# A fused cross-attention and mixture-of-experts kernel: the first loads over two queues, K of batch 0 by halves, and a block that closes without GpSimd's drain

## The chip, the core and the metric

The kernel runs as one program on one core of a Trainium2 chip. Its engines are TensorE (PE), VectorE (DVE), ScalarE (ACT), GpSimd (POOL) and SyncE (SP). They run their own instruction streams and meet at semaphores; DMAs are issued from the queues of SyncE, ScalarE and GpSimd. The metric is the device time of one execution in microseconds.

## The reference

x and the context have 4 batches of 512 tokens of 256 features, in f32. Every line below is computed.

```python
kv = (mem @ W_kv)                       # layernorm(x) and mem = ctx: 16 heads of 16
q = (x @ W_q)
attn = softmax(q k^T * HEAD_DIM ** -0.5)
x = x + tanh(g_xattn[0]) * ((attn @ v) @ W_proj + b_proj)
logits = xf @ gate_w.T                  # xf = layernorm(x), 2048 tokens, 8 experts
topk_logits, topk_idx = jax.lax.top_k(logits, 2)
topk_w = softmax(topk_logits)
for e in range(8):
    out = out + comb[:, e:e+1] * ((silu(xf @ wg[e].T) * (xf @ wu[e].T)) @ w_down[e].T)
x = x + tanh(g_ffn[0]) * (shared + out)  # shared: the same gated form with its own weights
```

## The kernel before

The program is one block in which each engine's instructions stand in an order written out by hand; nothing schedules them. It has three stages.

The first stage, some 60 us, loads ctx (already transposed on the host, `ctxT`), x and the attention weights, normalises x by batch, and makes K, V and Q of each batch. SyncE's queue carries the K half of `w_kv`, ctxT of batch 0, the V half, and then ctxT and x of batches 1 to 3. ScalarE's queue carries x of batch 0, `w_q`, the two gates, the bias, `w_proj` and the router weights. TensorE first runs `WARM` = 36 transposes of an identity tile whose result nobody reads (L1290). Then, for batches 0 and 1, it runs `project_k` (two output halves c, each a sum over two input halves d), half of `project_v`, `turn_xn` (eight transposes of the normalised rows `rows` into xnT, L1300), the other half of `project_v`, and `project_q`. All plain products go through the helper `mm` at L1284.

K and Q of batches 0 and 1 are each split into three bf16 parts. ScalarE makes the high part from PSUM (`high_k`, L701; `high_q`, L697), VectorE the residual (`resid_part`, L923), ScalarE the middle part (`mid_part`, L689), and VectorE the low part (`low_part`, L913). ScalarE also copies the turned rows (`copy_xnT`, L693) and V (`copy_v`, L709), takes standard deviations (`std_of`, L677) and, for batches 1 to 3, applies the normalisation (`apply_rows`, L683), all in one fixed order. Next to these VectorE has the statistics of x (`ln_stats`, L880 and L884), and for batch 0 the whole normalisation (`ln_apply`, ending at L894). `project_k(b, 0)` waits for ctxT of its batch (`ctx_in`) and, for batches 1 and 2, for the residual of the batch before, since both use the same PSUM banks. For batches 2 and 3 K and Q are copied whole (`whole_k`, L714; `whole_q`, L718). From batch 2 on, score tiles for the row maxima of the first unit (`first_pair`) stand between the products; VectorE reduces each pair (`max_pair`, L929), and from the third pair on TensorE waits for the maximum before last.

SyncE copies the parts of batch 0 into the units' operands (48 DMAs, `copy_rows`, L430, from the low part of K on), then stores the parts of batch 1 (L444), then sends the first row maxima (`send_max`, L457), for which the first unit's scores wait.

The second stage is the attention of 16 units (a batch and four heads), paced by TensorE. The third is projection, router, shared expert and 36 expert blocks. GpSimd adds each block's rows to `out` in HBM by indirect DMAs (L655). SyncE waits for all of them at the end (L502). At the block's end every engine drains, and all meet in a barrier (L143).

Of the kernel before, what the change touches and what calls it, by code (L numbers as in the profile page):

```python
# [22 lines left out]
P = 128  # L23
# [5 lines left out]
B, T, D = 4, 512, 256  # L29
N = B * T  # L30
NT = N // P
TB = T // P
DC = D // P
# [5 lines left out]
E, HALF, FFN = 8, 384, 768  # L39
# [45 lines left out]
ROW_HOMES = 8  # L85
EPS = 1e-5
GATE_W = P // TB
WARM = 36

K_RUNS = ((0, 1, 2), (0,), (0, 1))  # L90
Q_RUNS = ((0, 1), (0, 1, 2), (0,))
# [43 lines left out]
def build(nc, x, ctxT, g_xattn, g_ffn, w_kv, w_q, w_proj, b_proj, gateT, w_upT, w_downT, out):  # L135
# [4 lines left out]
    x_dram = x.rearrange("b (t p) d -> p (b t) d", p=P)  # L140
    out_dram = out[0:N, :].rearrange("(t p) d -> p t d", p=P)

    with ExitStack() as ctx:  # L143
        def sb(name, shape, dt=F32):
            return ctx.enter_context(nc.sbuf_tensor(name, shape, dt))

        def sem(name):
            return ctx.enter_context(nc.semaphore(name))

        x_sb = sb("x_sb", [P, NT, D])
# [3 lines left out]
        ctx_sb = ctx_region[:, :].rearrange("p (c n) -> p c n", c=DC)  # L155
# [5 lines left out]
        dn_region = sb("dn_region", [P, (E + 1) * FC * D])  # L161
        w_dn = dn_region[:, :].rearrange("p (e f n) -> p e f n", e=E + 1, f=FC)
        part_words = B * 2 * 3 * DC * T // 2
        parts = up_region[:, 0:part_words].bitcast(BF16).rearrange("p (b a j c n) -> p b a j c n", b=B, a=2, j=3, c=DC)
        resid = dn_region[:, 0:2 * DC * T].rearrange("p (a c n) -> p a c n", a=2, c=DC)
        v_words = TB * H * VW

        unit_words = 4 * HG * T + v_words
# [80 lines left out]
        wkv_sb = sb("wkv_sb", [P, DC, 2 * D])  # L249
        wp_sb = sb("wp_sb", [P, DC, D])  # L250
        gate_sb = sb("gate_sb", [P, DC, GATE_W])
        bias_sb = sb("bias_sb", [P, D])
# [3 lines left out]
        ident = sb("ident", [P, P])  # L256
# [47 lines left out]
        def bank(i, n=1):  # L304
            return ps[i // 4][:, i % 4, :] if n == 1 else ps[i // 4][:, i % 4:i % 4 + n, :]
# [4 lines left out]
        K_BANK, V_BANK = 4, 6  # L310
# [9 lines left out]

        x_in = [sem(f"x_in{b}") for b in range(B)]
        ctx_in = [sem(f"ctx_in{b}") for b in range(B)]
        wk_in, wv_in, wq_in = sem("wk_in"), sem("wv_in"), sem("wq_in")
        gates_in = sem("gates_in")
        small_in = sem("small_in")
        const_step = sem("const_step")
        gate_zero = sem("gate_zero")
# [16 lines left out]
        k_ps, v_ps, q_ps = sem("k_ps"), sem("v_ps"), sem("q_ps")  # L344
# [53 lines left out]
        out_done = sem("out_done")  # L398

        order_steps = [0]  # L400
        block = ctx.enter_context(nc.Block())

        @block.sync
        def _(sp):
            def load_ctx(b):
                sp.dma_start(ctx_sb[:, :, b * T:(b + 1) * T],
                             ctxT.rearrange("(c p) n -> p c n", p=P)[:, :, b * T:(b + 1) * T]).then_inc(ctx_in[b], 16)

            w_kv_rows = w_kv.rearrange("(c p) n -> p c n", p=P)  # L410
            sp.dma_start(wkv_sb[:, :, 0:D], w_kv_rows[:, :, 0:D]).then_inc(wk_in, 16)
            load_ctx(0)
            sp.dma_start(wkv_sb[:, :, D:2 * D], w_kv_rows[:, :, D:2 * D]).then_inc(wv_in, 16)
            for b in range(1, B):
                load_ctx(b)
                sp.dma_start(x_sb[:, b * TB:(b + 1) * TB, :], x_dram[:, b * TB:(b + 1) * TB, :]).then_inc(x_in[b], 16)

            def load_rows(b, g, a, dst, runs):
                row = 0
# [239 lines left out]

        @block.scalar  # L660
        def _(act):
            act.dma_start(x_sb[:, 0:TB, :], x_dram[:, 0:TB, :]).then_inc(x_in[0], 16)
            act.dma_start(wq_sb[:, :, :], w_q.rearrange("(c p) n -> p c n", p=P)).then_inc(wq_in, 16)
            act.dma_start(gates[:, 0:1], g_xattn.partition_broadcast(P)).then_inc(gates_in, 16)
            act.dma_start(gates[:, 1:2], g_ffn.partition_broadcast(P)).then_inc(gates_in, 16)
            act.dma_start(bias_sb[:, :], b_proj.partition_broadcast(P)).then_inc(small_in, 16)
            act.dma_start(wp_sb[:, :, :], w_proj.rearrange("(c p) n -> p c n", p=P)).then_inc(small_in, 16)
            act.wait_ge(gate_zero, 1)
            act.dma_start(gate_sb[:, :, 0:E], gateT.rearrange("(c p) n -> p c n", p=P)).then_inc(small_in, 16)

            def copy_first_max():
                act.wait_ge(nmT_ps, 1)
# [199 lines left out]

        @block.vector
        def _(dve):
            nc.vector.memset(gate_sb[:, :, :], 0.0).then_inc(gate_zero, 1)
            nc.vector.memset(eps_sb[:, :], EPS)

# [49 lines left out]
            def max_pair(w, p, s):  # L927
# [8 lines left out]
            nc.vector.tensor_copy(same_e_bf[:, :], same_e[:, :])  # L936
            nc.vector.tensor_copy(before_tile[:, :, :],
                                  same_e[:, :].unsqueeze(1).to_broadcast([P, NT, E])).then_inc(route, 1)
            dve.wait_ge(x_in[0], 16)
            ln_stats(0, 1)  # L940
            ln_apply(0, 1)
            resid_part(1, 0)
# [146 lines left out]
            for t in range(NT):  # L1089
                last = nc.vector.max(top8[:, t, :], logits[:, t, :])  # L1090
# [5 lines left out]
            for t in range(NT):  # L1096
                last = nc.vector.max_index(top8_idx[:, t, :], top8[:, t, :], logits[:, t, :])
# [3 lines left out]
            for k in range(TOPK):  # L1101
                last = nc.vector.tensor_tensor(onehot[:, k, :, :], topi[:, k, :].unsqueeze(2).to_broadcast([P, NT, E]),
                                               iota_e[:, :].unsqueeze(1).to_broadcast([P, NT, E]), ALU.is_equal)
# [73 lines left out]
            for i in range(TABLE_PARTS):  # L1177
                n = PAIRS // TABLE_PARTS
# [103 lines left out]
        def _(pe):  # L1282
            def mm(o_, w, m, start=True, stop=True):
                return nc.tensor.matmul(o_, w, m, start=start, stop=stop)  # L1284

            pe.wait_ge(ident_done, 1)

            for i in range(WARM):
                nc.tensor.transpose(bank(7)[:, 0:P], ident[:, :], ident[:, :])  # L1290

            def turn_xn(b):
                pe.wait_ge(rows_done, b + 1)
                if b == 1:
                    pe.wait_ge(rowsT_sb, 1)
                elif b >= 2:
                    pe.wait_ge(whole_sb, WHOLE_ORDER.index((1, b)) + 1)
                for t in range(TB):
                    for c in range(DC):
                        last = nc.tensor.transpose(bank(XT_BANK[b] + c)[:, t * P:(t + 1) * P],  # L1300
                                                   rows[:, b * TB + t, c * P:(c + 1) * P], ident[:, :])
                last.then_inc(rowsT_ps, 1)

            def project_q(b, c, chunks=range(DC)):
                if (c, chunks[0]) == (0, 0):
                    if b == 0:
                        pe.wait_ge(wq_in, 16)
                    pe.wait_ge(rowsT_sb, b + 1)
                    if b == 1:
                        pe.wait_ge(resid_done, QK_ORDER.index((0, 0)) + 1)  # L1310
                    elif b >= 2:
                        pe.wait_ge(v_done, b + 1)
                for d in chunks:
                    last = mm(bank(Q_BANK[b] + c), wq_sb[:, d, c * P:(c + 1) * P], xnT[:, d, b * T:(b + 1) * T],
                              d == 0, d == DC - 1)
                if (c, chunks[-1]) == (DC - 1, DC - 1):
                    last.then_inc(q_ps, 1)

            def project_k(b, c):
                if c == 0:  # L1320
                    if b == 0:
                        pe.wait_ge(wk_in, 16)
                    pe.wait_ge(ctx_in[b], 16)
                    if b in (1, 2):
                        pe.wait_ge(resid_done, QK_ORDER.index((1, b - 1)) + 1)
                    elif b == 3:
                        pe.wait_ge(rowsT_sb, 3)
                for d in range(DC):
                    last = mm(bank(K_BANK + c), wkv_sb[:, d, c * P:(c + 1) * P], ctx_sb[:, d, b * T:(b + 1) * T],
                              d == 0, d == DC - 1)  # L1330
                if c == DC - 1:
                    last.then_inc(k_ps, 1)

            def project_v(b, tiles):
                if tiles[0] == 0:
                    if b == 0:
                        pe.wait_ge(wv_in, 16)
                    elif b <= 2:
                        pe.wait_ge(v_done, b)
                    else:  # L1340
                        pe.wait_ge(whole_sb, WHOLE_ORDER.index((0, 2)) + 1)
                for kt in tiles:
                    for d in range(DC):
                        tok = b * T + kt * P
                        last = mm(bank(V_BANK + kt // 2)[:, (kt % 2) * D:(kt % 2 + 1) * D], ctx_sb[:, d, tok:tok + P],
                                  wkv_sb[:, d, D:2 * D], d == 0, d == DC - 1)
                if tiles[-1] == TB - 1:
                    last.then_inc(v_ps, 1)
# [61 lines left out]
                            max_tile(u + 2, kt * HG + i, w, lambda p: True)  # L1410
                    also(k)

            for b in range(2):
                project_k(b, 0)
                project_k(b, 1)
                project_v(b, (0, 1))
                turn_xn(b)
                project_v(b, (2, 3))
                project_q(b, 0)
                project_q(b, 1)  # L1420

            def first_pair(w, p):
                if p == 0:
# [363 lines left out]
```

## Time and profile before

| | us |
|---|---|
| median of 3 runs | 493.08 |
| the 3 runs | 493.06 to 493.8 |
| profiled execution | 493.61 |
| its span, first to last instruction | 491.9 |
| TensorE busy | 476.5 (97%) |
| VectorE, ScalarE, GpSimd busy | 305.9, 261.0, 183.9 |

The span is 1.71 us shorter than the profiled execution's own time. Busy shares are averages over stages; the change lies in the first 60 us and behind the last 10 us, so the rows further down come from those two places.

### The profile page before, as it was taken

Reading aid. Unit: us, or ns where it says so; the run is one execution under the profiler, and the core shown is the slowest. Engines: PE = TensorE matmul, PEld = TensorE weight load, DVE = VectorE, ACT = ScalarE, POOL = GpSimd, SP = SyncE. Lnnn points to the kernel's source line nnn. Section 1 sums busy time; section 2 is a strip of 40 time slices with the busy share of each in tenths; the row PEclk is TensorE's granted clock in tenths of the full one; section 3 lists DMA queues with packets and bytes.
Section 4 is the critical chain, followed back from the end, with each engine's and each line's share of the span. In section 5 each row is a group of like instructions: output and inputs, shape, how many; then the busy total and the mean of one; then the engine's idle time right before and its main releaser. Section 6 shows DMA issues by size and latency. Waiting matters only on the chain.

```text
span 491.9 us, 7745 instructions
## 1 busy us (share of the span) xinstructions
PE 476.5 (97%) x2783; PEld 286.3 (58%) x2783; DVE 305.9 (62%) x574; ACT 261.0 (53%) x416; POOL 183.9 (37%) x216
## 2 busy tenths in 40 slices
PE   8999999999999999999989999999999999999992
PEld 7665523333233233334446465699799799799992
DVE  3666779999899999996464699533333333333331
ACT  1665277777777777776544400306346346244430
POOL 4810178872231111111000023604547647767332
PEclk9999999999999999999999999999999999999997
DMA  7733408866753565211104001322334525445232
GB/s 246 236 102 105 138 7 228 218 182 183 212 147 87 159 165 163 65 34 55 33 24 149 1 2 43 113 93 46 63 53 65 76 45 87 65 63 78 33 33 32
DMA packets 36741, 48.30 MB, mean 98 GB/s; under 512 B 6240, under 2 KB 29920, under 8 KB 36704
## 3 DMA queue, kind: packets, MB, share of 16 engines
q1 hardware_dynamic: 21536, 26.16, 18.8%
q0 software_dynamic: 7344, 9.84, 13.1%
q10 hardware_dynamic: 7824, 11.81, 7.6%
q8 instruction: 23, 0.38, 0.4%
q14 instruction: 14, 0.11, 0.1%
HBM read 30.16 MB, written 14.29 MB: 90 GB/s over the span
## 4 chain that ended last, share of the span: by engine, by line
PE 94%; DVE 3%; ACT 1%; issue 1%; POOLq 0%; POOL 0%
PE ps L1284 73%; PE ps L1370 13%; PE ps L1646 2%; PE ps L1657 2%; PE ps L1290 1%; PE ps L1679 1%; DVE rows L894 1%; DVE neg_max L929 1%; ACT ctx_region L763 1%; PE ps L1300 1%; PE ps L1362 0%; PE ps L1518 0%; PE ps L1527 0%; POOLq L143 0%; DVE stats L880 0%
## 5 line engine op out<-in xcount | busy, mean ns | idle before, releaser
L763 ACT ACTIVATE ctx_region<-ps 128x512 f32<-128x512 f32 x256 | 140.7, 594 | 47.5 <-PE ps L1284 47.5
L929 DVE TENSOR_REDUCE neg_max<-ps 128x2 f32<-128x1024 f32 x128 | 151.0, 1209 | 21.5 <-PE ps L1284 19.6
L1284 PE MATMUL ps<-unit_region 96*128 96x512 bf16 (+1 forms) x512 | 128.4, 380 | 1.2 <-ACT ctx_region L763 0.7
L1284 PEld LDWEIGHTS ps<-unit_region 96*128 96x128 bf16 (+1 forms) x512 | 45.0, 97 | 101.4 <-ACT ctx_region L763 45.2
L1284 PE MATMUL ps<-unit_region,ctx_region 128*128 128x128 f32 (+1 forms) x824 | 97.4, 274 | 0.0
L1284 PEld LDWEIGHTS ps<-unit_region,ctx_region 128*128 128x128 f32 (+1 forms) x824 | 94.3, 188 | 0.7 <-DVE x_sb L1071 0.3
L655 POOL DMA_INDIRECT out<-unit_region x39 | 61.2, 1570 | 54.2 <-DMA out<-unit_region 31.0
L1284 PE MATMUL ps<-dn_region,unit_region 128*128 (+1 forms) x294 | 70.0, 381 | 0.0
L844 ACT COPY ctx_region<-up_region 128x1536 f32 x33 | 48.5, 1472 | 34.8 <-PE ps L1284 27.2
L1241 DVE TENSOR_TENSOR unit_region<-unit_region,ps 128x384 f32<-128x384 f32 x35 | 19.4, 555 | 71.5 <-ACT unit_region L861 62.6
L1284 PEld LDWEIGHTS ps<-dn_region,unit_region 128*128 128x128 f32 x294 | 53.2, 190 | 8.4 <-issue 2.8
L861 ACT ACTIVATE unit_region<-ps 128x384 f32<-128x384 f32 x36 | 17.6, 490 | 63.5 <-PE ps L1284 59.2
L1370 PE MATMUL ps<-ctx_region,dn_region 128*32 128x512 f32 x384 | 51.1, 605 | 0.0
L622 POOL DMA_INDIRECT rows<-x_rows,unit_region x36 | 36.0, 1000 | 34.5 <-DMA out<-x_sb 13.5
L578 POOL CAST nm_parts<-nmT 16x128 bf16<-16x128 f32 x16 | 4.5, 280 | 114.8 <-ACT nmT L755 100.6
L1284 PE MATMUL ps<-xnT,up_region 128*128 128x512 f32 x96 | 42.6, 595 | 0.0
L1262 DVE TENSOR_SCALAR unit_region<-ps,unit_region 128x256 f32<-128x256 f32 x36 | 17.4, 484 | 27.2 <-PE ps L1284 23.3
L628 POOL TENSOR_TENSOR unit_region<-ctx_region,unit_region 128x1248 bf16<-128x1248 bf16 x3 | 8.0, 2652 | 63.1 <-DVE ctx_region L1163 63.0
L1284 PEld LDWEIGHTS ps<-xnT,up_region 128*128 128x128 f32 x96 | 17.8, 190 | 19.8 <-issue 19.7
L805 ACT ACTIVATE unit_region<-ps 128x512 f32<-128x512 f32 x12 | 7.0, 596 | 28.6 <-PE ps L1284 28.6
L1370 PEld LDWEIGHTS ps<-ctx_region,dn_region 128*32 128x32 f32 x384 | 7.5, 108 | 18.9 <-ACT ctx_region L763 14.9
L1370 PE MATMUL ps<-ctx_region,unit_region 128*32 128x512 f32 x128 | 17.0, 605 | 0.8 <-ACT ctx_region L763 0.8
(200 smaller groups left out, 464.8 us busy)
## 6 DMA issues: line engine op xcount, KB each, us to landing
up_region<-in_w_upT ACTq DMA_DIRECT2D x9, 768.0 KB, 4.5
qk_parts<-up_region SPq DMA_DIRECT2D x24, 192.0 KB, 3.2
unit_region<-qk_parts SPq DMA_DIRECT2D x24, 192.0 KB, 4.1
dn_region<-in_w_downT ACTq DMA_DIRECT2D x9, 384.0 KB, 5.3
unit_region<-up_region SPq DMA_DIRECT2D x48, 64.0 KB, 2.6
unit_region<-qk_parts SPq DMA_DIRECT2D x24, 128.0 KB, 4.1
ctx_region<-in_ctxT SPq DMA_DIRECT2D x4, 512.0 KB, 10.4
x_rows<-rows SPq DMA_DIRECT2D x4, 512.0 KB, 3.9
```

Of the source, the lines that this page charges most:

```text
L622: pool.indirect_dma_start(out=blk_x[:, home, :], out_offset=None, in_=x_rows[:, :], in_offset=bass.IndirectOffsetOnAxis(ap=blk_token[:, AD ...
L655: pool.indirect_dma_start(out=out[:, :], out_offset=bass.IndirectOffsetOnAxis(ap=blk_row[:, a:a + 1], axis=0), in_=blk_y[:, j % Y_HOMES, : ...
L763: nc.scalar.activation(probs[:, k % 8, :], bank(SCORE_HOME[u, k]), ACT.Exp).then_inc(exp_done, 1)
L844: nc.scalar.copy(up_now[:, n % 2, :, :].rearrange("p c f -> p (c f)"), w_up[:, bass.ds(chosen_expert.pop(a), 1), :, :].rearrange("p a c f ...
L861: nc.scalar.activation(blk_gate[:, :], bank(2 * (j % 2))[:, 0:HALF], ACT.Silu).then_inc(bsilu, 1)
L929: nc.vector.tensor_reduce(neg_max[:, s, 2 * p:2 * p + 2], bank(2 * (p % 2), 2), AX.X, ALU.max, negate=True).then_inc(max_done, 1)
L1241: nc.vector.tensor_tensor(blk_h[:, s, :], blk_gate[:, :], bank(2 * s + 1)[:, 0:HALF], ALU.mult).then_inc(bhid, 1)
L1262: nc.vector.tensor_scalar(blk_y[:, j % Y_HOMES, :], bank(6 + s)[:, 0:D], blk_weight[:, ADDS_OF[j][0]:ADDS_OF[j][0] + 1], None, ALU.mult).t ...
L1284: return nc.tensor.matmul(o_, w, m, start=start, stop=stop)
L1370: last = nc.tensor.matmul(bank(6)[h * VW:(h + 1) * VW, :], v_home(u // NG)[:, kt, u % NG * HG + h, :], probs[:, (kt * HG + h) % 8, :], sta ...
L1646: last = nc.tensor.transpose(bank(4)[:, c * P:(c + 1) * P], blk_x[:, s, c * P:(c + 1) * P], ident[:, :])
L1657: nc.tensor.matmul(bank(2 * s + g)[0:HALF_P, 0:HALF], blk_xT[:, s, c, 0:HALF_P], w_up[:, bass.ds(expert[ADDS_OF[j][0]], 1), c, cols].rearr ...
```

## The change

(2) SyncE's queue starts with ctxT of batch 0 in two halves by input feature, each with its own semaphore, then the first tile of x, then the V weights. (3) ScalarE's queue starts with the K weights in two halves, then the other three tiles of x of batch 0; the bias, `w_proj` and the router weights move to SyncE, behind its other loads and ahead of the copies. (4) The first K products run by input half: both output halves for d = 0, then both for d = 1, in two PSUM banks. (5) The warm-up is nine plain f32 matmuls of a zeroed 128x128 piece of `dn_region`, behind a memset of VectorE, in place of 36 transposes of the identity. (6) V of batch 0 is made in one piece ahead of the turn of xn. (7) K of batch 1 is split: its first output half goes between the turn and Q of batch 0, its second behind Q.

```diff
-WARM = 36
+WARM = 9
-        block = ctx.enter_context(nc.Block())
+        block = ctx.enter_context(nc.Block(no_gpsimd_drain=True))
...
-            sp.dma_start(wkv_sb[:, :, 0:D], w_kv_rows[:, :, 0:D]).then_inc(wk_in, 16)
-            load_ctx(0)
-            sp.dma_start(wkv_sb[:, :, D:2 * D], w_kv_rows[:, :, D:2 * D]).then_inc(wv_in, 16)
+            for c in range(DC):
+                sp.dma_start(ctx_sb[:, c, 0:T], ctxT[c * P:(c + 1) * P, 0:T]).then_inc(first_ctx_in[c], 16)
+            sp.dma_start(x_sb[:, 0:1, :], x_dram[:, 0:1, :]).then_inc(x_in[0], 16)
+            sp.dma_start(wkv_sb[:, :, D:2 * D], w_kv.rearrange("(c p) n -> p c n", p=P)[:, :, D:2 * D]).then_inc(wv_in, 16)
...
+            sp.dma_start(bias_sb[:, :], b_proj.partition_broadcast(P)).then_inc(small_in, 16)
+            sp.dma_start(wp_sb[:, :, :], w_proj.rearrange("(c p) n -> p c n", p=P)).then_inc(small_in, 16)
+            sp.wait_ge(gate_zero, 1)
+            sp.dma_start(gate_sb[:, :, 0:E], gateT.rearrange("(c p) n -> p c n", p=P)).then_inc(small_in, 16)
...
-            act.dma_start(x_sb[:, 0:TB, :], x_dram[:, 0:TB, :]).then_inc(x_in[0], 16)
+            for c in range(DC):
+                act.dma_start(wkv_sb[:, c, 0:D], w_kv[c * P:(c + 1) * P, 0:D]).then_inc(wk_in[c], 16)
+            act.dma_start(x_sb[:, 1:TB, :], x_dram[:, 1:TB, :]).then_inc(x_in[0], 16)
...
+            nc.vector.memset(warm[:, :], 0.0).then_inc(warm_set, 1)
...
-            dve.wait_ge(x_in[0], 16)
+            dve.wait_ge(x_in[0], 16 * 2)
...
+            pe.wait_ge(warm_set, 1)
+            for i in range(WARM):
+                mm(bank(7)[:, 0:P], warm[:, :], warm[:, :])
             pe.wait_ge(ident_done, 1)
-
-            for i in range(WARM):
-                nc.tensor.transpose(bank(7)[:, 0:P], ident[:, :], ident[:, :])
...
+            def project_first_k():
+                for d in range(DC):
+                    pe.wait_ge(wk_in[d], 16)
+                    pe.wait_ge(first_ctx_in[d], 16)
+                    for c in range(DC):
+                        last = mm(bank(K_BANK + c), wkv_sb[:, d, c * P:(c + 1) * P], ctx_sb[:, d, 0:T], d == 0, d == DC - 1)
+                last.then_inc(k_ps, 1)
```

On TensorE, from its first instruction to Q of batch 0, this stood in the program before (`ident` is the identity tile, `wkv_sb` the K and V weights, `ctx_region` ctxT, `xnT` the turned rows):

```order
L1290 MATMUL ps<-ident 128x128 [waits ident_done]
L1290 MATMUL ps<-ident 128x128 x35
L1284 MATMUL ps<-ctx_region,wkv_sb 128x512 [waits ctx_in0,wk_in]
L1284 MATMUL ps<-ctx_region,wkv_sb 128x512 x3
L1284 MATMUL ps<-wkv_sb,ctx_region 128x256 [waits wv_in]
L1284 MATMUL ps<-wkv_sb,ctx_region 128x256 x3
L1300 MATMUL ps<-ident,rows 128x128 [waits rows_done]
L1300 MATMUL ps<-ident,rows 128x128 x7
L1284 MATMUL ps<-wkv_sb,ctx_region 128x256 x4
L1284 MATMUL ps<-xnT,wq_sb 128x512 [waits rowsT_sb,wq_in]
```

And this stands there now, on the same engine, up to the second half of K of batch 1:

```order
L1290 MATMUL ps<-dn_region 128x128 [waits warm_set]
L1290 MATMUL ps<-dn_region 128x128 x8
L1290 MATMUL ps<-ctx_region,wkv_sb 128x512 [waits first_ctx_in0,wk_in0,ident_done]
L1290 MATMUL ps<-ctx_region,wkv_sb 128x512
L1290 MATMUL ps<-ctx_region,wkv_sb 128x512 [waits first_ctx_in1,wk_in1]
L1290 MATMUL ps<-ctx_region,wkv_sb 128x512
L1290 MATMUL ps<-wkv_sb,ctx_region 128x256 [waits wv_in]
L1290 MATMUL ps<-wkv_sb,ctx_region 128x256 x7
L1306 MATMUL ps<-ident,rows 128x128 [waits rows_done]
L1306 MATMUL ps<-ident,rows 128x128 x7
L1290 MATMUL ps<-ctx_region,wkv_sb 128x512 [waits resid_done,ctx_in1]
L1290 MATMUL ps<-ctx_region,wkv_sb 128x512
```

The turn of the rows (L1300, now L1306) has moved behind all eight V products, and the first half of K of batch 1, with its wait for the residual, has moved ahead of Q.

On SyncE's queue, the first loads stood like this, up to the first copy of the parts:

```order
L411 DMA wkv_sb<-in_w_kv 128x2x256
L407 DMA ctx_region<-in_ctxT 128x2x512
L413 DMA wkv_sb<-in_w_kv 128x2x256
L407 DMA ctx_region<-in_ctxT 128x2x512
L416 DMA x_sb<-in_x 128x4x256
L407 DMA ctx_region<-in_ctxT 128x2x512
L416 DMA x_sb<-in_x 128x4x256
L407 DMA ctx_region<-in_ctxT 128x2x512
L416 DMA x_sb<-in_x 128x4x256
L430 DMA unit_region<-up_region 16x4x512 [waits low_done]
```

Now the same queue has:

```order
L414 DMA ctx_region<-in_ctxT 128x512 x2
L415 DMA x_sb<-in_x 128x256
L416 DMA wkv_sb<-in_w_kv 128x2x256
L410 DMA ctx_region<-in_ctxT 128x2x512
L419 DMA x_sb<-in_x 128x4x256
L410 DMA ctx_region<-in_ctxT 128x2x512
L419 DMA x_sb<-in_x 128x4x256
L410 DMA ctx_region<-in_ctxT 128x2x512
L419 DMA x_sb<-in_x 128x4x256
L420 DMA bias_sb<-in_b_proj 128x256
L421 DMA wp_sb<-in_w_proj 128x2x256
L423 DMA gate_sb<-in_gateT 128x2x8 [waits gate_zero]
```

The K weights have left this queue for ScalarE's, a tile of x stands ahead of the V weights, and three loads of ScalarE's queue stand at its end.

## Rows read from the trace of the kernel before

**Rows 1.** The page: the chain that ended last, its shares of the span by engine.

```profile
PE 94%; DVE 3%; ACT 1%; issue 1%; POOLq 0%; POOL 0%
```

**Rows 2.** The chain in order of time: start us, us, engine and line; first and later pieces.

```profile
1.58 6.83 PE ps L1290 x36
8.41 5.16 PE ps L1284 x16
...
37.71 11.22 PE ps L1284 x36
```

**Rows 3.** The timeline, 0 to 12 us: start us, us, engine, line, operation.

```profile
0.89 0.11 DVE L875 MEMSET gate_sb<- 128x64 f32 x1 [0.89 <-PEq L1780]
...
1.31 0.45 SPq L407 DMA_DIRECT2D ctx_region<-in_ctxT  x1
...
5.74 1.41 DVE L880 BATCH_NORM_STATS2 stats<-x_sb 128x6 f32<-128x256 f32 x4 [3.46 <-DMA x_sb<-in_x]
...
8.14 1.38 DVE L894 TENSOR_SCALAR rows<-x_sb,mean_var,rstd 128x256 f32<-128x256 f32 x4
...
8.25 3.60 PE L1284 MATMUL ps<-ctx_region,wkv_sb 128*128 128x512 f32 x8
...
11.69 1.89 PE L1284 MATMUL ps<-wkv_sb,ctx_region 128*128 128x256 f32 x8
```

**Rows 4.** Warm-up alone: busy time in one window, and its weight loads, 6 to 6.5 and 7.2 to 8 us.

```profile
2.00:6.90 4.90, 4.90 (x25) 4.90 (x24) 1.00 0.92 306
...
L1290 PEld LDWEIGHTS ps<-ident 128*128 128x128 f32 x3 | 0.7, 230 | 0.0
...
L1290 PEld LDWEIGHTS ps<-ident 128*128 128x128 f32 x8 | 0.9, 140 | 0.0
```

**Rows 5.** Windows from the start; the last numbers are clock, DMA share and GB/s.

```profile
0.00:4.10 4.10, 2.52 (x12) 2.52 (x13) 0.81 (x5) 0.00 (x0) 2.74 (x14) 1.00 0.40 123
0.00:5.50 5.50, 3.92 (x19) 3.92 (x20) 0.81 (x5) 0.25 (x1) 2.86 (x14) 1.00 0.57 188
0.00:6.30 6.30, 4.72 (x22) 4.72 (x23) 1.37 (x7) 1.05 (x1) 2.86 (x14) 1.00 0.63 208
```

**Rows 6.** DMA issues of 0 to 1.5 us: size, us from issue to landing.

```profile
x_sb<-in_x ACTq DMA_DIRECT2D x1, 512.0 KB, 4.9
ctx_region<-in_ctxT SPq DMA_DIRECT2D x1, 512.0 KB, 6.3
wkv_sb<-in_w_kv SPq DMA_DIRECT2D x1, 256.0 KB, 3.8
```

**Rows 7.** The timeline, ScalarE's copy of the turned rows of batch 0.

```profile
14.49 1.01 ACT L693 COPY xnT<-ps 128x1024 f32<-128x1024 f32 x1 [1.59 <-PE ps L1300]
```

**Rows 8.** The timeline, 29 to 43 us: ScalarE, VectorE and TensorE around the first maxima.

```profile
29.19 2.08 ACT L683 ACTIVATE rows<-x_sb,shift,rstd 128x256 f32<-128x256 f32 x4 [0.44 <-DVE shift L908]
...
35.75 3.66 DVE L929 TENSOR_REDUCE neg_max<-ps 128x2 f32<-128x1024 f32 x3
...
37.55 0.60 PE L1284 MATMUL ps<-unit_region 96*128 96x512 bf16 x2
...
42.50 1.23 DVE L929 TENSOR_REDUCE neg_max<-ps 128x2 f32<-128x1024 f32 x1 [0.93 <-PE ps L1284]
```

**Rows 9.** The end, by line: count, ns min/median/max, first and last start.

```profile
L502 SPq EVENT_SEMAPHORE  x2: 17/22/28, 487.8 to 487.8; - x2
...
L143 POOLq DRAIN  x1: 7968/7968/7968, 483.7 to 483.7; - x1
...
L143 SPq DRAIN  x1: 7/7/7, 488.1 to 488.1; - x1
```

**Rows 10.** The timeline: SyncE's queue from 17 us, and TensorE's last max tiles and first scores.

```profile
17.73 31.26 SPq L430 DMA_DIRECT2D unit_region<-up_region  x48
...
54.50 14.48 SPq L457 DMA_DIRECT2D unit_region<-nm_parts  x6
...
60.90 1.03 PE L1284 MATMUL ps<-unit_region 96*128 96x512 bf16 x4
```

More of the change, by code:

```diff
@@ L165, in build @@
         resid = dn_region[:, 0:2 * DC * T].rearrange("p (a c n) -> p a c n", a=2, c=DC)
+        warm = dn_region[:, 0:P]
         v_words = TB * H * VW
@@ L322, in build @@
         ctx_in = [sem(f"ctx_in{b}") for b in range(B)]
-        wk_in, wv_in, wq_in = sem("wk_in"), sem("wv_in"), sem("wq_in")
+        first_ctx_in = [sem(f"first_ctx_in{c}") for c in range(DC)]
+        wk_in = [sem(f"wk_in{c}") for c in range(DC)]
+        wv_in, wq_in, warm_set = sem("wv_in"), sem("wq_in"), sem("warm_set")
         gates_in = sem("gates_in")
@@ L408, in load_ctx @@
                              ctxT.rearrange("(c p) n -> p c n", p=P)[:, :, b * T:(b + 1) * T]).then_inc(ctx_in[b], 16)
-            w_kv_rows = w_kv.rearrange("(c p) n -> p c n", p=P)
-            sp.dma_start(wkv_sb[:, :, 0:D], w_kv_rows[:, :, 0:D]).then_inc(wk_in, 16)
-            load_ctx(0)
-            sp.dma_start(wkv_sb[:, :, D:2 * D], w_kv_rows[:, :, D:2 * D]).then_inc(wv_in, 16)
+            for c in range(DC):
+                sp.dma_start(ctx_sb[:, c, 0:T], ctxT[c * P:(c + 1) * P, 0:T]).then_inc(first_ctx_in[c], 16)
+            sp.dma_start(x_sb[:, 0:1, :], x_dram[:, 0:1, :]).then_inc(x_in[0], 16)
+            sp.dma_start(wkv_sb[:, :, D:2 * D], w_kv.rearrange("(c p) n -> p c n", p=P)[:, :, D:2 * D]).then_inc(wv_in, 16)
             for b in range(1, B):
@@ L665, in _ @@
             act.dma_start(gates[:, 1:2], g_ffn.partition_broadcast(P)).then_inc(gates_in, 16)
[L666 to L669, printed above, removed]
             def copy_first_max():
@@ L1317, in project_q @@
                     last.then_inc(q_ps, 1)
+            def project_first_k():
[5 more added lines that the diff above has]
+                last.then_inc(k_ps, 1)
             def project_k(b, c):
                 if c == 0:
-                    if b == 0:
-                        pe.wait_ge(wk_in, 16)
                     pe.wait_ge(ctx_in[b], 16)
@@ L1411, in slot @@
                     also(k)
[L1413 to L1420, printed above, removed]
+            project_first_k()
+            project_v(0, (0, 1))
+            project_v(0, (2, 3))
+            turn_xn(0)
+            project_k(1, 0)
+            project_q(0, 0)
+            project_q(0, 1)
+            project_k(1, 1)
+            project_v(1, (0, 1))
+            turn_xn(1)
+            project_v(1, (2, 3))
+            project_q(1, 0)
+            project_q(1, 1)
             def first_pair(w, p):
```

## The prediction

> **What bounds the kernel now.** I read the chain that ended last first. It gives TensorE 94% of 491.9 us [rows 1], so only two kinds of time are to be had: time before TensorE's first useful product, and time after its last. In order of time the chain starts with the 36 warm-up transposes (1.58 to 8.4 us) and goes straight into the K products of batch 0. From there to 48.9 us TensorE has no gap, apart from pieces that the chain gives to itself [rows 2]. The rows of the first microseconds show what the start waits for: the warm-up itself. The last piece that the K products need, ctxT of batch 0, is issued at 1.31 and lands 6.3 us later, at 7.6; the K products begin at 8.25 behind the last transpose [rows 3, 6]. At the other end the last scatter-add has landed by 487.8 us, where SyncE's wait ends, and SyncE's own drain is over at 488.1. But the drain of GpSimd runs from 483.7 for 7.97 us, to 491.7, and the closing barrier stands behind it [rows 9]. The profiled execution took 493.61 us, 1.71 more than its span and 0.53 more than the median of the three runs.
>
> **The closing step.** The new program has no such drain for GpSimd; the other four keep theirs. What is late next is SyncE at 488.1; its wait for all scatter-adds stays. In the old program 0.2 us passes between the drain's end (491.7) and the end of the span, and I keep that: 488.3 in place of 491.9, a gain of **3.6 us**. Bounds: 3.6 if nothing outside the span takes over, and 0 if what follows the kernel has to do the same drain. I take 3.6, since every byte has landed and no row after 487.8 shows work. The Trainium skill ("Runtime: NRT & Kernel Launch", The ~15µs preamble/postamble breakdown) has a barrier and a DMA re-arm behind every kernel. By that page GpSimd might be waited for there, and the gain would be 0; no row here shows that stretch.
>
> **The start of TensorE.** Cold, the transposes follow each other every 0.213 us (25 records of 0.42 us overlap 4.9 us), later about twice as fast; their weight loads go from 230 to 140 ns, and 36 records in 6.57 us fit 25 slow ones, so TensorE went from 1.2 to 2.4 GHz at about 7.1 us [rows 3, 4]. (The profile's clock column has 1.00 for all of it and does not tell the two apart.) The new warm-up is nine plain f32 matmuls. A plain f32 matmul leaves two records (four K products are eight [rows 3]), so 18 records, 18 x 0.213 = 3.85 us. They wait for a small memset of VectorE, whose first one starts at 0.89, not for ident at 1.52: start about 1.1, end about 5.0.
>
> **The first loads.** Counting bytes by stretches of the windows view, 504 KB had moved by 4.1 us, 1034 by 5.5, 1310 by 6.3 [rows 5]. x of batch 0 (512 KB, alone at the head of ScalarE's queue) landed at 5.7, when 1.1 MB had moved in all, so the two queues shared about equally, and a landing shows 0.2 to 0.6 us behind its bytes (the first weights, issued at 0.80, took 3.8 us; their 256 KB are through at about 4.1) [rows 5, 6]. New order: SyncE has a 256 KB ctxT half, the second half, one x tile, V weights; ScalarE has two 128 KB weight halves, three x tiles, wq. So the first halves are in at about 4.6, the second at about 5.9, x of batch 0 (640 KB on each queue) at about 6.7, 1 us later than before, V weights (896 KB) at about 8.5. K can start right behind the warm-up, at 5.0, and its second half, wanted at 7.5 at the earliest, never waits. The Trainium skill ("DMA: Bandwidth & Descriptors", Issuing engines are not separate DMA queues) says that transfers issued by several engines run on the same 16 DMA engines and interleave. By it the second queue brings no bandwidth at all. The rows agree: both queues together stay at about the rate of the windows [rows 5], and my landings use that rate; what changes is only which bytes go first.
>
> **K and what follows it.** K takes 3.44 us at the high clock (8.25 to 11.69 [rows 3]). Started at 5.0 with the rise at 7.1, half of those 2.1 us is lost: K ends at 5.0 + 3.44 + 1.05 = 9.5, **2.2 us** earlier. The rise may come 1.5 us either way (the trace has one sample): 0.75 each way. All eight V products now run before the turn of xn: 12.95. The turn (0.87) wants the normalised rows: VectorE needed 3.8 us from the landing of x to the end of its rows (5.74 to 9.52 [rows 3]), so 10.5, early enough. It ends at 13.8; before, the copy of the turned rows on ScalarE began at 14.49 [rows 7], now about 14.05. So ScalarE and VectorE are ahead by 0.45 only, TensorE by 2.2, and the slack between them shrinks. Moving K(1, 0) behind the turn covers that copy: it ends at 15.1, Q wants it at 15.5. I followed the order of both engines with the durations of the old rows. Q of batch 0 ends at 19.0, its high part on ScalarE at 20.7, the residual at 22.0, copy_xnT(1) at 25.0, just when TensorE wants it (25.05). The residual of K(1) is through at 25.6 and its mid part at 26.7 (before 27.64), so apply_rows(2) runs from 28.25 (before 29.19). From there ScalarE is ahead by 0.9: the high part of Q(1) right behind it, and the first row maximum at VectorE from 34.95 (before 35.8, three of them in 3.66) [rows 8]. TensorE, 2.1 ahead, is at the turn of batch 2 by 34.55 and at its third pair of score tiles by 35.45. That pair waits for the first maximum, 1.2 us long: 36.2. Before, it began at 37.55 [rows 8]. **So 0.8 us of the 2.1 is given back to VectorE's first maxima; 1.3 stays.** From there on the distances stay, since TensorE with its products between the pairs is slower per pair than VectorE, which waited 0.93 us for it between maxima of 1.23 [rows 8].
>
> **SyncE.** It issues from 17.73 without a pause: 48 copies to 49.0, 8 stores, and then the three rows of maxima from 54.5, which land about 2.6 us later each, the last near 58 [rows 10]. The moved loads (bias, wp, gate) stand ahead of the copies; bytes in all are the same, and the queue must be free by 17.3, when the low part of K is due. Before, its last initial issue was over at 9.6; I expect 13 to 14. The first scores stand right behind the last max tiles, at about 61.3 [rows 10], now 60.0: still 2 us of slack. No cost. ScalarE is free of these three issues sooner; its table load only moves ahead. bias is first read behind the maxima of the second unit and wp in the last units, far later. No cost either.
>
> **Sum.** 493.61 - 3.6 - 1.3 = 488.7 against the profiled execution, 488.2 against the median. I say 488.4.
>
> **Rivals.**
> (a) The front gain stays whole: the rise of the clock comes early, or VectorE's maxima don't hold. 2.1 to 2.6 us: 487.3. For it: before, no wait at all showed there. Against: the third pair began at 37.55 and the first maximum was over by 37.0 [rows 8], a distance of 0.6 us.
> (b) The front gain is lost: x lands at 9 or later instead of 6.7, or the rise comes near 9, and ScalarE's chain starts no earlier than now. 489.6 to 489.9.
> (c) The drain comes back behind the span. The span shrinks to 487, the time does not: 493.3 - 1.3 = 492.0.
> (d) Both (b) and (c): 493.2, no change.
> (e) Slower: TensorE's clock stays at 1.2 GHz much longer, since the K, V and turn work now has gaps around the loads where an unbroken row of 36 transposes stood. With the rise at c the useful work done by c is (c - 5.0)/2 against c - 8.25 before; less 3.6 for the end, it is slower from c = 18.7 us on, and with (c) from c = 11.5 on. At c = 14 with (c): 494.3. Against: TensorE is busy without a gap from 1.1 to the turn by my landings.
>
> **How the numbers follow.** Forecast (487.8 to 489.1) 0.54; (a) 0.16; (b) 0.10; (c) 0.12; (d) 0.04; (e) 0.04. A measurement of this kernel can tell about 0.2%, 1 us, from no change. Faster: forecast, (a), (b), (c) = 0.92; same: (d) = 0.04; slower: 0.04. Without (c) to (e), 0.2 is left out, so the range is 486.6 to 490.4, which takes in (b) and an early rise.
>
> **What would show it.** Right: no long GpSimd drain at the end, span ending 0.5 us behind SyncE's last wait, time minus span still 1.7; K products from about 5.0, half speed until about 7; a wait of TensorE on VectorE's maximum near 35.5. Wrong: time minus span of 5 us (c); a wait of TensorE ahead of the turn of xn (b); weight loads of 230 ns in the V products (e); maxima for the first scores landing after 60 (SyncE late).

## The result, and the profile after

| | before | after |
|---|---|---|
| median | 493.07 us | 488.72 us |
| runs | 492.94 to 493.8 | 488.55 to 488.92 |
| ratio, 95% interval | | 0.9909 (0.9892 to 0.9926) |
| profiled execution | 493.61 us | 488.55 us |
| its span | 491.9 us | 486.5 us |
| time minus span | 1.71 us | 2.05 us |

The kernel is 4.35 us faster, 0.9%. I had forecast 488.4 between 486.6 and 490.4.

First the end, which answers to [rows 9]. These are rows of the kernel after by line, with count, ns and start:

```profile
L143 POOLq EVENT_SEMAPHORE  x2: 17/17/17, 486.3 to 486.4; - x2
...
L143 SPq DRAIN  x1: 7/7/7, 486.2 to 486.2; - x1
```

GpSimd has no drain any more. SyncE's drain starts at 486.2, and the last semaphore instruction stands at 486.4. Before, 3.8 us lay between SyncE's drain (488.1) and the end of the span; now it is 0.3.

Then the first microseconds, the timeline of the kernel after, which answers to [rows 3] and [rows 7]:

```profile
1.12 4.20 PE L1290 MATMUL ps<-dn_region 128*128 128x128 f32 x18 [1.12 <-DVE dn_region L880]
...
5.71 3.67 PE L1290 MATMUL ps<-ctx_region,wkv_sb 128*128 128x512 f32 x8 [0.40 <-DMA wkv_sb<-in_w_kv]
...
8.98 1.41 DVE L886 BATCH_NORM_STATS2 stats<-x_sb 128x6 f32<-128x256 f32 x4 [6.70 <-DMA x_sb<-in_x]
...
9.77 3.72 PE L1290 MATMUL ps<-wkv_sb,ctx_region 128*128 128x256 f32 x16 [0.39 <-DMA wkv_sb<-in_w_kv]
...
11.38 1.38 DVE L900 TENSOR_SCALAR rows<-x_sb,mean_var,rstd 128x256 f32<-128x256 f32 x4
...
13.33 1.04 PE L1306 MATMUL ps<-ident,rows 128*128 128x128 f32 x8
...
14.40 1.01 ACT L698 COPY xnT<-ps 128x1024 f32<-128x1024 f32 x1 [2.38 <-PE ps L1306]
```

K starts 2.54 us earlier than before (8.25), at 5.71. But x lands 3.2 us later (8.98 against 5.74), the V products wait for their weights until 9.77, and the turn of xn at 13.33 is where it was (13.41). ScalarE's copy of the turned rows starts at 14.40 against 14.49.

And the place where TensorE meets VectorE's first maxima, the timeline of the kernel after from 32 to 38.5 us, which answers to [rows 8]:

```profile
34.43 0.60 PE L1290 MATMUL ps<-unit_region 96*128 96x512 bf16 x2
34.87 1.04 PE L1306 MATMUL ps<-ident,rows 128*128 128x128 f32 x8
34.97 3.48 DVE L935 TENSOR_REDUCE neg_max<-ps 128x2 f32<-128x1024 f32 x3
...
36.24 0.60 PE L1290 MATMUL ps<-unit_region 96*128 96x512 bf16 x2 [0.33 <-DVE neg_max L935]
```

The third pair of score tiles starts at 36.24, 1.31 us earlier than before (37.55), and behind a wait for VectorE's first maximum that the kernel before did not have.

The difference of the two profiled executions, 5.06 us, has four parts that the rows show: 1.31 at the start; about 0.4 from a stall near 130 us that only the execution of before has (last section); 3.5 at the end of the span; less 0.34 that shows between span and time. They add up to 4.9; where the other 0.1 to 0.2 lies I did not find.

### The profile page after: what moved, and what is told of

The parts are those of the page before. It is cut to its first block, busy times and chain, and to the rows that moved or that the text cites. A ratio compares the mean times of both kernels' runs of the same rounds, so it can differ in the third digit from the quotient of the medians.

```text
span 486.5 us, 7717 instructions
## 1 busy us (share of the span) xinstructions
PE 474.4 (98%) x2765; PEld 283.5 (58%) x2765; DVE 305.7 (63%) x575; ACT 260.9 (54%) x416; POOL 183.9 (38%) x216
## 4 chain that ended last, share of the span: by engine, by line
PE 88%; DVE 5%; ACT 3%; DMA 2%; issue 1%; POOL 0%; SPq 0%; POOLq 0%
PE ps L1290 69%; PE ps L1382 13%; PE ps L1663 2%; PE ps L1674 2%; DMA wkv_sb<-in_w_kv 2%; DVE neg_max L935 1%; PE ps L1696 1%; ACT up_region L694 1%; ACT rows L688 1%; DVE dn_region L929 1%; DVE rows L900 1%; ACT ctx_region L768 1%; PE ps L1374 0%; PE ps L1535 0%; PE ps L1544 0%
```

## The experiments

All kernels of the study have one addition: GpSimd checks the bounds of the counts that it loads for its scatter-adds. The first run is the kernel before with that addition, the second the changed kernel. They are the two controls. The kernels came in three groups, each with the kernel before measured beside it: its median was 492.93 us beside the first four, 492.68 beside the next four (old order, old loads, whole operands, V weights first) and 492.74 beside the last four. So a difference of 0.2 us between kernels of different groups can be one of the groups.

**Control of before.** 

> The kernel before with one addition that all kernels of this study have: GpSimd checks the bounds of the counts that it loads for the scatter-adds. A control. If that addition lies off the path, 493.1 us (492.9 to 493.8). If GpSimd is on the path between the scatter-adds, up to 1 us more.

Measured: 493.26 us (ten runs, 492.73 to 493.68); the kernel before itself beside it 492.93. Ratio 1.0005 (0.9995 to 1.0014). The addition costs nothing that can be measured. In its profile K starts at 7.82, not at 8.25, right behind the landing of ctxT (7.7), since TensorE's weight loads went to the high clock at 5.9 us and not at 7.1: the old warm-up ends a little earlier or later from execution to execution.

**Control of after.** 

> The changed kernel with the same addition, a control. 488.7 us, and 4.35 below the control of before. The 0.5 us stall of TensorE near 130 us that the profiled execution of before shows and that of after doesn't is by chance, if it is in one of these two profiles or in neither, whichever.

Measured: 488.77 us (488.3 to 488.88), 4.49 below the control of before. The stall near 130 us is in this profile, although it is not in the one of the changed kernel.

**The closing step alone.**

```diff
-        block = ctx.enter_context(nc.Block())
+        block = ctx.enter_context(nc.Block(no_gpsimd_drain=True))
```

> The kernel before, and only the closing step without GpSimd's drain. My theory (two separate gains, 3.55 in the span at the end less 0.35 that shows outside it, 1.3 at the start): 489.85, span 488.3, time minus span 2.05. Rival (the end is worth all of it, and what TensorE gained at the start is swallowed before the end): 488.7.

Measured: 489.43 us (489.05 to 490.27), ratio to before 0.9925 (0.9909 to 0.9942): 3.8 us below the control, 0.7 above the changed kernel. The rows of its end by line:

```profile
L502 SPq EVENT_SEMAPHORE  x2: 17/22/28, 487.9 to 487.9; - x2
...
L143 SPq DRAIN  x1: 7/7/7, 488.2 to 488.2; - x1
```

The span is 488.4: it ends 0.5 us behind SyncE's last wait. Time minus span was 1.76 to 1.87 in its four runs, against 1.73 to 1.88 in the ten of the control. So nothing took over outside the span. This is rival (c) of the prediction, and it falls. The 0.34 of the two profiled executions is not all scatter, though. Time minus span is 1.77 in the mean of the control of before, 1.82 in the mean of each of the two kernels that have one part of the change, and 1.86 to 2.01 in the means of the ten kernels that have both. Some 0.1 to 0.2 us of the gain in the span is thus lost outside it once both parts are in. What it goes to no row shows.

**The start alone**: the changed kernel with `nc.Block()`. 

> The changed kernel, but GpSimd drains again at the end. My theory: 491.8, time minus span 1.7, a drain of GpSimd that ends 3.6 us behind SyncE's last wait. Rival (the end is worth all of it): 493.1, no change.

Measured: 492.30 us (ten runs, 492.0 to 492.53), ratio 0.9986 (0.9976 to 0.9996), 0.96 below the control of before. The two rows at its end:

```profile
L509 SPq EVENT_SEMAPHORE  x2: 17/22/28, 486.1 to 486.2; - x2
...
L143 POOLq DRAIN  x1: 7972/7972/7972, 482.3 to 482.3; - x1
```

The drain took 7.97 us again, from 482.3 to 490.2, and ended 4.0 us behind SyncE's wait. It took 7.97 in the profiles of before and of the control too. I had expected 491.8, and the start alone brought less than that. By medians the closing step is worth 3.83 us against the control of before and 3.53 on top of the start; the start is worth 0.96 and 0.66. The two single parts come to 4.8 that way and both together to 4.49, but by the means of the runs they add up: 3.61 and 0.87 alone, 4.47 together. The start brings less in the median than the 1.3 of the profiled pair, because that execution of before had one of the later starts of K (8.25; the others 7.82 and 8.45) and this one of after one of the earlier third pairs (36.24; the others 36.39 and 36.66). Over three profiles of either start the third pair moves from 37.50 to 36.43 in the mean: 1.07 us.

**The order of before on TensorE.**

```diff
             project_first_k()
             project_v(0, (0, 1))
-            project_v(0, (2, 3))
             turn_xn(0)
-            project_k(1, 0)
+            project_v(0, (2, 3))
             project_q(0, 0)
             project_q(0, 1)
+            project_k(1, 0)
             project_k(1, 1)
```

> The changed kernel with TensorE's order of before for batches 0 and 1: the turn of xn between the halves of V, Q of batch 0 ahead of both halves of K of batch 1. My theory (x lands at 8.9, so the rows are ready at 12.75, and TensorE idles between the first half of V at 11.5 and the turn): turn 0.5 us earlier than 13.33, but 1.3 us of TensorE idle; TensorE then binds instead of VectorE's first maxima, third pair of score tiles at 36.9 instead of 36.24: 489.3, 0.6 over the changed kernel. Rival (the order is worth nothing, VectorE's maxima bind either way): 488.7 or 0.4 less.

Measured: 489.08 us (488.91 to 489.67), 0.3 over the changed kernel's control. Against the kernel before in its own group it is 3.60 faster, the control 4.16, which makes it 0.56. The order of V and the turn and the place of K of batch 1 are undone together here. Its timeline:

```profile
9.90 1.99 PE L1289 MATMUL ps<-wkv_sb,ctx_region 128*128 128x256 f32 x8 [0.54 <-DMA wkv_sb<-in_w_kv]
12.89 1.09 PE L1305 MATMUL ps<-ident,rows 128*128 128x128 f32 x8 [0.99 <-DVE rows L899]
```

The turn comes 0.6 us earlier than in the control (12.89 against 13.48), and TensorE idles ahead of it, for the rows. The third pair is at 37.09, as expected (36.9), with no wait for the maximum: TensorE's own work sets it. My 489.3 was right within its scatter. In this profile the new order hides the late x: in the old one TensorE idles 0.99 us for the rows.

**The loads of before**, with the new order and warm-up: whole K weights, ctxT and V weights on SyncE, x of batch 0 first on ScalarE, the small loads on ScalarE.

> The changed kernel with the loads of before (whole K weights, whole ctxT and V weights on SyncE's queue, x of batch 0 at the head of ScalarE's, small loads on ScalarE's). K products can start only at 7.6 with ctxT. My theory (x at 5.7 and V weights at 8.8 are earlier than in the changed kernel, K later): K 7.6 to 11.05, V to 14.5, turn to 15.4, 1.1 us later than in the changed kernel; the first maxima and the third pair follow: 489.9. Rival (the split and the second queue gained nothing, because the V weights come 0.9 earlier here): 488.7.

Measured: 491.42 us (nine runs, 491.07 to 493.08), 1.5 over my expectation. The timeline shows why:

```profile
8.05 6.16 PE L1287 MATMUL ps<-ctx_region,wkv_sb 128*128 128x512 f32 x8 [2.72 <-DMA ctx_region<-in_ctxT]
14.05 3.62 PE L1287 MATMUL ps<-wkv_sb,ctx_region 128*128 128x256 f32 x16
```

K takes 6.0 us (8.05 to 14.05) and not 3.44. The nine warm-up products end at 5.3, TensorE then idles 2.7 us for ctxT, and the weight loads of its products are slow until 13 us: 337 ns each between 11 and 13, 190 after 13.2.

```profile
L1287 PEld LDWEIGHTS ps<-ctx_region,wkv_sb 128*128 128x128 f32 x3 | 1.0, 337 | 1.5 <-issue 1.5
...
L1287 PEld LDWEIGHTS ps<-wkv_sb,ctx_region 128*128 128x128 f32 x1 | 0.2, 190 | 0.2 <-issue 0.2
```

TensorE was at 1.2 GHz for K up to about 13 us: the mechanism of rival (e), in a kernel where the gap stands. But the profiled execution took 492.48, one of three late ones (492.14, 492.48, 493.08); the other six took 491.07 to 491.69. K lost 2.6 us in it, and 489.9 and 2.6 are its 492.5. The median lost only 1.5 us, so in most executions K must have lost less, for instance by an earlier rise of the clock; no profile shows one of them.

**The same loads with 18 warm-up products** (`WARM = 18`). 

> The changed kernel with the loads of before, as in the run with the old loads, and 18 warm-up products instead of 9 (36 records, as many as before), so that TensorE has work until ctxT lands near 7.6 to 8. In that run TensorE idled 2.7 us ahead of K and its weight loads went to the high clock only at 13.07 us. Theory (the idle stretch kept the clock low, and this cost most of the 1.5 us by which that run missed my 489.9): high clock between 4 and 8 us, K from about 8, V from 11.5, turn at 15, 489.8 to 490.2. Rival (the old loads themselves cost 2.7 us): 491.4.

Measured: 490.23 us (489.45 to 490.43).

```profile
1.12 7.03 PE L1287 MATMUL ps<-dn_region 128*128 128x128 f32 x36 [1.12 <-DVE dn_region L877]
7.98 3.60 PE L1287 MATMUL ps<-ctx_region,wkv_sb 128*128 128x512 f32 x8
```

Same loads, no gap, K at full speed in 3.44 us (7.98 to 11.42). 1.2 of the 1.5 us are back, so the clock explains most of the miss. What is left over the changed kernel, 1.5 us (490.23 against 488.77; 1.65 by groups), is what the new loads are worth behind the new order.

That is more than the whole start is worth, and four kernels without the drain show why (the kernels of the new order or the new loads have the new warm-up; in brackets the gain over the kernel before in the same group):

| | old order | new order |
|---|---|---|
| old loads | 489.43 (3.50) | 490.23 (2.51) |
| new loads | 489.08 (3.60) | 488.77 (4.16) |

Behind the old loads the new order costs 0.8 to 1.0 us: the turn of xn stands behind all of V and starts at 14.87, where it starts at 13.62 with the closing step alone. In the old order the new loads bring 0.1 to 0.35 us. Only both together bring 0.7. So neither edit can be priced by taking it out of the finished kernel.

**No warm-up** (`WARM = 0`). 

> The changed kernel without any warm-up. K starts at 5.6 to 5.7, when its weights land, in any case. Theory (the warm-up brings the high clock forward; it came 3.2 to 6.4 us behind the first product in the runs without a gap): high clock at 9 to 12 us, K ends at 10.8 to 12.2 in place of 9.15, V behind it; the turn comes 1 to 2.5 us later: 489.8 to 491.2. Rival (K is covered by the wait for the V weights, which ends at 9.77): 489.2 or less.

Measured: 489.82 us (489.73 to 490.9), 1.05 over the control.

```profile
5.91 5.48 PE L1289 MATMUL ps<-ctx_region,wkv_sb 128*128 128x512 f32 x8 [5.91 <-DMA wkv_sb<-in_w_kv]
11.23 3.62 PE L1289 MATMUL ps<-wkv_sb,ctx_region 128*128 128x256 f32 x16
```

K takes 5.3 us and V starts at 11.23 in place of 9.93: its weight loads are slow until about 9.6 us. The loss is more than the wait for the V weights covers. The 6.4 us in my range stands in no profile that I had; the latest rise of the clock without a gap was about 5.8 us behind the first product, in the kernel with the closing step alone.

**K operands loaded whole.**

```diff
-            for c in range(DC):
-                sp.dma_start(ctx_sb[:, c, 0:T], ctxT[c * P:(c + 1) * P, 0:T]).then_inc(first_ctx_in[c], 16)
+            sp.dma_start(ctx_sb[:, :, 0:T], ctxT.rearrange("(c p) n -> p c n", p=P)[:, :, 0:T]).then_inc(first_ctx_in[0], 16)
...
-            for c in range(DC):
-                act.dma_start(wkv_sb[:, c, 0:D], w_kv[c * P:(c + 1) * P, 0:D]).then_inc(wk_in[c], 16)
+            act.dma_start(wkv_sb[:, :, 0:D], w_kv.rearrange("(c p) n -> p c n", p=P)[:, :, 0:D]).then_inc(wk_in[0], 16)
```

> The changed kernel with ctxT of batch 0 and the K weights loaded whole, each by one DMA, at the same places of the same queues. In the changed kernel 242 GB/s moved from 4 to 5 us where 386 moved before, and x landed 2.2 us later than I had forecast. Theory A (several small DMAs at the head of a queue fill the 16 engines worse than two large ones): x lands near 7 to 7.5, V weights near 8.6, K starts near 5.9 to 6.3; time 488.2 to 488.5. Theory B (the order of the bytes is the cause, 2 KB rows of ctxT at the head of one queue run slow whether whole or by halves): x at 8.9 as in the changed kernel, K 0.3 us later, time 488.7 to 488.9.

Measured: 488.76 us (488.08 to 490.22), x at 8.25 in place of 8.98. The windows of 3 to 4 and 4 to 5 us (the last two numbers are the busy share of the DMA engines and GB/s), first the kernel before, then this one, then the changed kernel:

```profile
3.00:4.00 1.00, 1.00 (x7) 1.00 (x6) 0.00 (x0) 0.00 (x0) 0.79 (x4) 1.00 0.92 300
4.00:5.00 1.00, 1.00 (x6) 1.00 (x5) 0.00 (x0) 0.00 (x0) 0.15 (x2) 1.00 1.11 386
```

```profile
3.00:4.00 1.00, 1.00 (x6) 1.00 (x6) 0.00 (x0) 0.29 (x1) 0.79 (x4) 1.00 0.93 267
4.00:5.00 1.00, 1.00 (x7) 1.00 (x5) 0.00 (x0) 1.00 (x1) 0.15 (x2) 1.00 0.87 235
```

```profile
3.00:4.00 1.00, 1.00 (x6) 1.00 (x6) 0.00 (x0) 0.00 (x0) 0.79 (x4) 1.00 0.89 183
4.00:5.00 1.00, 1.00 (x7) 1.00 (x5) 0.00 (x0) 0.78 (x1) 0.15 (x2) 1.00 0.92 242
```

Neither theory holds alone. Of the 3.2 us by which x lands later than before, 0.7 go with the halves; the rest stays with whole loads, so it belongs to the order of the bytes and to the slow stretch from 3 to 5 us. From 3 to 4 us the DMA engines are as busy as before (0.93 and 0.89 against 0.92) and move less; from 4 to 5 they are less busy too (0.87 and 0.92 against 1.11). The single DMA packets in the traces show where the time goes. ctxT moves in packets of 2 KB, at the head of SyncE's queue in both new orders. In the changed kernel one took 161 ns on average from 3 to 4 us and 130 from 4 to 5, and 99 from 5 to 6; in the kernel before, where ctxT moved from 4 us on, one took 84 to 97 ns. The packets of 1 KB took 46 to 62 ns from 4 to 6 us in all three kernels. So the slow bytes are those of ctxT while it moves first, whole or by halves. Why they are slow there no row shows. In the profiled execution TensorE had again idled (1.11 us) ahead of K and ran it slowly (6.44 to 11.77), and it took 490.22. The other three took 488.08 to 488.78 with the same loads and the same warm-up, so the gap does not always cost this.

**The same with 12 warm-up products.** 

> The changed kernel with ctxT of batch 0 and the K weights loaded whole (x landed at 8.25 there, 0.7 earlier than with halves) and 12 warm-up products instead of 9, to cover the wait for them until 6.45. Theory (with the gap closed the clock is high from 4 to 8 us on; K ends at 9.9, V at 13.3, the turn is where the changed kernel has it, since the end of V sets it and the rows at 12.0 are early): 488.5 to 488.8, so the halves of K are worth little here. Rival (the rows and x set the turn, not V): 488.1.

Measured: 488.62 us (488.48 to 488.86): the same as the control. K runs at full speed from 6.57 to 10.08, and the turn is at 13.54 (control 13.48). So with the longer warm-up the halves of K bring nothing that lasts. The end of V sets the turn, and starting K 0.9 us later moves the start of V by only 0.15 us.

**V weights ahead of the x tile.** 

> The changed kernel with the V weights ahead of the x tile on SyncE's queue. In the changed kernel TensorE waits from 9.2 to 9.77 for the V weights. My theory: they land some 0.5 us earlier, V runs 9.3 to 12.75, the turn starts at 12.85 to 13.0 behind the rows: third pair of score tiles is held by VectorE's first maximum, whose chain starts at low parts and not at this turn, so little of it is kept: 488.4 to 488.7. Rival (everything follows the end of V): the whole 0.5 us, 488.2.

Measured: 488.99 us (488.85 to 489.02), 0.2 over the control and 0.3 over the slower end of my expectation. V starts at 9.25 without a wait, but the x tile lands later and the turn waits for the rows:

```profile
9.25 3.62 PE L1289 MATMUL ps<-wkv_sb,ctx_region 128*128 128x256 f32 x16
13.58 1.09 PE L1305 MATMUL ps<-ident,rows 128*128 128x128 f32 x8 [0.71 <-DVE rows L899]
```

Both my theory and its rival had expected an earlier turn. They overlooked that the x tile pays: x went from 9.06 in the control to 9.74.

**A short first maximum.**

```diff
+                cols = P if (w, p) == (0, 0) else T
-                nc.vector.tensor_reduce(neg_max[:, s, 2 * p:2 * p + 2], bank(2 * (p % 2), 2), AX.X, ALU.max,
+                nc.vector.tensor_reduce(neg_max[:, s, 2 * p:2 * p + 2], bank(2 * (p % 2), 2)[:, :, 0:cols], AX.X, ALU.max,
```

> The changed kernel, but the first row maximum of the first unit reads 128 of its 512 columns, so about 0.35 us in place of 1.2. Left out is the maximum over the other 384 columns of two tiles (the softmax only uses it as a shift). My prediction had TensorE wait there. In the trace of the changed kernel TensorE is done with the turn of batch 2 at 35.74 and starts the third pair at 36.24. Theory (VectorE's first maximum holds TensorE): third pair at 35.75, all that follows 0.5 us earlier, 488.2. Rival (the next wait, for the second maximum or for ScalarE's whole_k, takes its place): third pair earlier, but first exponential at 60.7 as before, 488.7.

Measured: 488.27 us (487.9 to 488.8), 0.5 below the control. Its timeline:

```profile
34.90 0.60 PE L1290 MATMUL ps<-unit_region 96*128 96x512 bf16 x2
35.33 1.04 PE L1306 MATMUL ps<-ident,rows 128*128 128x128 f32 x8
...
36.21 0.60 PE L1290 MATMUL ps<-unit_region 96*128 96x512 bf16 x2
```

From the second to the third pair it is 1.31 us and no wait, against 1.81 in the changed kernel. In this profile everything ahead was 0.45 us later (V at 10.24; the clock rose between 7.0 and 7.35 us), so the start of the third pair is not itself earlier; the distance is, by 0.5. The 0.5 us is kept: from the second pair to the first exponential it is 25.78 us (34.90 to 60.68), against 26.28 (34.43 to 60.71), so the rival, in which the next wait takes it back, falls. The median points the same way, but the runs of the two kernels overlap (487.9 to 488.8 and 488.3 to 488.88), and by groups the difference is 0.3. VectorE's first maximum does take 0.5 us of TensorE's gain.

## Why the prediction was right

The closing step: forecast 3.6, measured 3.5 in the profiled span, 3.5 to 3.8 by the experiments. Its lower bound, nothing, and with it rivals (c) and (d), is ruled out by the kernel with that edit alone. I had named a time minus span of 1.7 as a sign of being right; it is 1.86 to 2.05 in the four runs of the changed kernel, a small loss that the prediction did not have.

The start: forecast 1.3, measured 1.31 in the profiled pair and 0.7 to 1.0 by medians. The agreement to 0.01 is luck of the two executions; the whole change was forecast at 4.7 us by medians and measured at 4.35. The mechanism is the one forecast. The chain that I had followed holds nearly to the end: apply_rows(2) at 28.41 (forecast 28.25), the first maximum at 34.97 (34.95), the third pair at 36.24 (36.2). Three terms ahead of it were mis-sized, and it was luck that they offset one another:

- K at 5.0, measured 5.71. The first halves landed at 5.4 to 5.6 and not at 4.6. K's halves in fact waited for a landing, 0.4 us. The second half of the K weights landed at about 7.2 and not at 5.9. In this profile that was just in time; in the control and in the start alone K's row is 0.1 and 0.3 us longer for it (3.75 and 3.98 against 3.67).
- The rise of the clock at 7.1. In this profile the last slow weight load (333 ns) ends at 5.03 and the next, K's first at 5.68, is fast (186 ns); in the control the rise is at about 4.6, in the start alone between 5.04 and 5.45. So K lost nothing to it. K ended at 9.15 (forecast 9.5).
- x at 6.7, measured 8.98, and the V weights at 8.5, measured 9.7. I had taken the byte count of the old windows for the new order, and the new order moved 183 and 242 GB/s where the old moved 300 and 386. The lateness of x was covered, since the rows (12.76) were only wanted at the end of V (13.2; forecast 12.95). The V weights were not covered: TensorE waited 0.6 us for them.

What TensorE gave back to VectorE was forecast at 0.8 us and measured at 0.5: at the second pair TensorE was 1.81 us ahead, not 2.1. The kernel after has its second pair at 34.43 (above); this is the one of the kernel before:

```profile
36.24 0.60 PE L1284 MATMUL ps<-unit_region 96*128 96x512 bf16 x2
```

Rival (a), in which nothing is given back, falls with the wait at 36.24 and with the kernel of the short maximum.

SyncE was no bound: its initial issues were over at 14.0 (forecast 13 to 14), its copies started at 17.64 (17.3), and its maxima went out from 54.47:

```profile
17.64 31.29 SPq L437 DMA_DIRECT2D unit_region<-up_region  x48
48.97 5.45 SPq L451 DMA_DIRECT2D qk_parts<-up_region  x8
54.47 2.07 SPq L464 DMA_DIRECT2D unit_region<-nm_parts  x3
```

Rival (b) needed x at 9 or later. It landed at 8.98 in the changed kernel and at 9.06 in its control, and TensorE still did not wait for the rows ahead of the turn of xn: the rows had more slack than I had written into (b). Rival (e) needed a gap in TensorE's work. The changed kernel has one of 0.4 us, and its weight loads were fast by 5.7 us in its profile, its control's and that of the start alone. In the kernel with the short maximum, which has the same start, they were slow until 7.0, and K's row was 4.38 us long and not 3.67. So a late rise did cost 0.7 us of K in one profile of this start.

## What to carry to other kernels

Look at what every engine does at the end of a program as closely as at its start: one drain of GpSimd, off every page of busy times, was worth some four fifths of this gain. When loads are dealt out anew, the rate of the old order is no rate of the new one; say what each later consumer loses (here x and the V weights) and keep slack behind them. Loads and the order of the work that uses them belong together: here each was worth little or less than nothing without the other. A gain of one engine at the start is kept only up to the first meeting with a chain that did not move, so follow the other engines' order to that meeting and size the gain there.

## What the runs showed that I had not expected

TensorE's clock rose at quite different times with the same warm-up. With nine warm-up products (from 1.12 us, over by 4.9 to 5.3) and no more than 0.64 us of idle time behind them, five profiles have the rise between 4.1 and 5.7 us, three of them inside the warm-up, and one has it between 7.0 and 7.35. With 18 products and no gap it was 6.9, with 12 and a gap of 0.64 it was about 5. In the two profiles with a longer gap it came late: 1.1 us of idle time and about 10.1, 2.7 us and about 13, which is 3.7 and 5.0 us behind the first K product; without any warm-up it came 3.7 us behind it. In these two the warm-up had done nothing for K. Closing the larger gap brought K back to full speed and the median down by 1.2 us. But each is one profiled execution, and the faster ones of the same kernels show that the gap alone does not decide it.

TensorE sometimes stalls 0.2 to 0.4 us near 130 us, with nothing to wait for that the profile shows. The row in the waits of TensorE from 126 to 133 us, in the kernel before:

```profile
PE ps L1284 <- issue: 0.4, 1, 0.4
```

The control of after and the kernel with the closing step alone have it too (0.3 us each), and the one with old loads and 18 warm-up products has 0.2; the changed kernel, the control of before and the other eight have not. Of the two pairs of before and after, one has it in before and the other in after, so it goes with the execution and not with the change, and it is as large as many edits.

GpSimd's closing drain took 7.97 us in each of the three profiles that I read it in, and ended 3.8 to 4.0 us after SyncE's wait for the last scatter-add had ended. What it does in that time no row shows.
